# A head's row maxima turned in mid-step, its first product with v in halves, and the maximum of the two halves on GpSimd

## The chip, the core and the metric

The kernel runs on one core of one Trainium2 chip. The core has five engines that run side by side and meet at semaphores: TensorE (PE, with its weight loads shown as PEld), VectorE (DVE), ScalarE (ACT), GpSimd (POOL) and SyncE (SP), which here issues all DMAs. The metric is the device time of one execution in microseconds (us), and lower is better.

## The reference

The layer normalises x (4 sequences of 2048 tokens, 256 wide), and adds to x an attention and a feed-forward branch. The part that matters here is attention with 16 heads of 16 values:

```
qkv = einsum('bld,ed->ble', x, w_qkv);  q, k, v = split(qkv)
q = rope(q);  k = rope(k)
scores = einsum('blhd,bmhd->bhlm', q, k) * scale
attn = softmax(scores, axis=-1)
out = einsum('bhlm,bmhd->blhd', attn, v).reshape(B, L, D)
return einsum('bld,ed->ble', out, w_out)
```

The softmax needs the maximum of each row of scores before its exponentials. There are 4 x 16 = 64 pairs of sequence and head, called heads below, with 2048 x 2048 scores each.

## The kernel before, in words

The first stage (some 540 us) makes normalised x, q, k, v and the feed-forward branch, and stages q and k in HBM as pairs of fp16 numbers. The second stage, attention, is the one that the change touches. It walks 1024 + 32 steps, c = 0, 1, ...; 16 steps (TILES) make a head. Three things run in one step, for three different places in the sequence of tiles:

- The maxima, for tile c. `max_half(c, i, half)` makes 1024 scores of 128 rows in banks 0 and 1 or 2 and 3 of PSUM (two matmuls, L659), and DVE reduces them to one number per row (L1222, `row_max`). PE may write a pair of banks again when DVE has read it (`s1_used`).
- The scores that are turned, for tile c - 19 (FIRST2 = TILES + LAG): four matmuls of 512 columns (L717) with rows added to q, the stabiliser, that subtract the maximum. They go to banks 4, 5, 6 in turn, a ring of three (`take_bank`, `s2_used`), and ACT takes the exponential of each (L828, `probs`).
- The product with v, for tile c - 21: `weigh_v(0)` and `weigh_v(1)`, each 256 columns of four blocks (L699), summed over a head in bank 7.

The order on PE in a step is: max_half 0, scores 0 and 1, weigh_v(0), max_half 1, scores 2 and 3, weigh_v(1). One such half of a step is called a half below. PE works strictly in this order, so an instruction that waits holds all behind it.

Twice per head something else comes in. **Place A** is step c = 16h + 17 (STAB_AT), the second of the next head. DVE has reduced the two halves of `row_max` to `neg_max` (L1212), GpSimd has scaled and split it into three fp16 parts with five small operations (`split_max`, L916 to L927), and PE turns these by a transpose (L678) right behind max_half 0. ACT copies the turned rows to `stabT` (L820), and SP writes them by two DMAs into `q_op` (L438). The scores of step 16h + 19 need them (`stab_loaded`). The transpose counts as two items of the ring of banks (STAB_ITEMS). **Place B** is step 16h + 37 (SAVE_AT): ACT copies the finished sum of head h out of bank 7 (L814, `acc_saved`), before its exponentials of that step. The next head's first product may not write bank 7 before that; in the kernel before it is not cut in two, and stands as one product of 512 columns at the end of the step.

Each engine's part of the program is written out in this order by `step`, without a scheduler.

Of the kernel before, what the change touches and what calls it, by code (L numbers as in the profile page):

```python
# [28 lines left out]
P = 128  # L29
DH = 16  # L30
BANK = 512
# [12 lines left out]
STAB_STEPS = 5  # L44
# [8 lines left out]
UNROLL = SLOTS * TILES  # L53
# [20 lines left out]
def layer_program(nc, x, w_qkv, w_out, w_gate, w_up, w_down, cos_tab, sin_tab, ident_in, out, y_dram, qk_dram, inv_dram):  # L74
# [48 lines left out]
    neg_max = sb(keep, "neg_max", [P, TILES])  # L123
# [3 lines left out]
    unit = sb(keep, "unit", [P, TILES])  # L127
# [149 lines left out]
    max_ready = sem("max_ready")  # L277
# [26 lines left out]

    STAB_ITEMS = 2
    HEAD_ITEMS = 4 * TILES + STAB_ITEMS
    assert HEAD_ITEMS % RING == 0

# [12 lines left out]
    def before(g, at):  # L321

        return min(max((g - at + TILES - 1) // TILES, 0), HEADS)

    def items_before(g):

        return 4 * min(max(g - FIRST2, 0), N1) + STAB_ITEMS * before(g, STAB_AT)

    def extra_items(g):

        return STAB_ITEMS * (head_of(g, STAB_AT) is not None)

    def run_steps(step):

        for c in range(STEPS_B):
            step(c, 0)
# [21 lines left out]
    def _(sp):  # L358
# [71 lines left out]
        def load_stab(hl, i):  # L430
            h = hl + SLOTS * i


            g = TILES * hl + STAB_AT
            sp.wait_ge(s2_used, items_before(g) + STAB_ITEMS + HEAD_ITEMS * SLOTS * i)
            for r in (0, HALF):
                dst = q_op[r + ROWS:r + ROWS + STAB_PARTS, hl % SLOTS, :].rearrange("a (t n) -> a t n", t=TILES)
                sp.dma_start(dst, stabT[:, :]).then_inc(stab_loaded, 16)  # L438
# [31 lines left out]
        for h in range(HEADS):  # L470
            load_stab(h, 0)
# [22 lines left out]
    def _(pe):  # L494
# [131 lines left out]
        pe.wait_ge(b_const, 6)  # L626
# [20 lines left out]
        def max_half(c, i, half):  # L647

            hl, t = divmod(c, TILES)
            if t == 0 and half == 0:  # L650
                pe.wait_ge(qk_loaded[hl % SLOTS], 16 * QK_LOADS * (hl // SLOTS + 1 + i))
            n = 2 * c + half
            if n >= 2:
                pe.wait_ge(s1_used, n - 1 + 2 * UNROLL * i)
# [8 lines left out]
        def step(c, i):  # L663
            item = items_before(c)

            def take_bank(item):

                if item >= RING:
                    pe.wait_ge(s2_used, item - RING + 1 + HEAD_ITEMS * SLOTS * i)
# [12 lines left out]

            def weigh_v(part):

                g3 = g2 - PV_LAG
                if 0 <= g3 < N1:
                    h, t = divmod(g3, TILES)

                    if t == 0 and part == 0:
                        return  # L690
                    if t == 0:
                        pe.wait_ge(v_ready, h + 1 + SLOTS * i)
                        if h >= 1:
                            pe.wait_ge(acc_saved, h + SLOTS * i)
                    if t == 0 or part == 0:
                        pe.wait_ge(s2_used, items_before(c - PV_LAG + 1) + HEAD_ITEMS * SLOTS * i)
                    n0, n1 = (0, BANK) if t == 0 else (part * (BANK // 2), (part + 1) * (BANK // 2))
                    for j in range(4):
                        mm = pe.matmul(bank(7)[32 * j:32 * j + 32, n0:n1], v_op[:, h % 2, t, :],  # L699
                                       probs[:, g3 % PROBS, j * BANK + n0:j * BANK + n1],  # L700
                                       start=(t == 0), stop=(t == TILES - 1 and part == 1), tile_position=(0, 32 * j))
# [3 lines left out]
            for j in range(4):  # L705
                if j == 2:
                    weigh_v(0)
                    if c < N1:
                        max_half(c, i, 1)
                if 0 <= g2 < N1:  # L710
                    h, t = divmod(g2, TILES)
                    if t == 0 and j == 0:
                        pe.wait_ge(stab_loaded, 32 * (h + 1 + SLOTS * i))
# [18 lines left out]
    def _(act):  # L732
# [69 lines left out]
        def step(c, i):  # L802
            item = items_before(c)

            def arrived(item, n=1):
                act.wait_ge(s2_full, item + n + HEAD_ITEMS * SLOTS * i)
# [3 lines left out]
            if h is not None:  # L810
                act.wait_ge(pv_done, TILES * (h + 1 + SLOTS * i))
                if h >= 2:
                    act.wait_ge(o_placed, 64 * (h - 1 + SLOTS * i))
                nc.scalar.activation(acc_sb[:, h % 2, :], bank(7), ACT.Copy).then_inc(acc_saved, 1)  # L814
            h = head_of(c, STAB_AT)
            if h is not None:
                if h >= 1:
                    act.wait_ge(stab_loaded, 32 * (h + SLOTS * i))
                b = arrived(item, STAB_ITEMS)
                nc.scalar.activation(stabT[:, :], bank(b).bitcast(F16)[0:STAB_PARTS * TILES, 0:P], ACT.Copy).then_inc(s2_used, STAB_ITEMS)  # L820
                item += STAB_ITEMS
            g2 = c - FIRST2
            if 0 <= g2 < N1:
                if g2 >= PROBS:
                    act.wait_ge(pv_done, g2 - PROBS + 1 + UNROLL * i)
                for j in range(4):
# [9 lines left out]
    def _(pool):  # L836
# [18 lines left out]
        nc.gpsimd.memset(unit[:, :], 1.0 / STAB_ONE).then_inc(b_const, 1)  # L855
        pool.wait_ge(b_const, 6)
# [55 lines left out]
        def split_max(h, first):  # L912

            n = STAB_STEPS * h
            pool.wait_ge(max_ready, h + 1)
            nc.gpsimd.tensor_tensor(neg_unit[:, :], neg_max[:, :], unit[:, :], ALU.mult).then_inc(stab_step, 1)  # L916
# [3 lines left out]
            pool.wait_ge(stab_step, n + 1)  # L920
            nc.gpsimd.tensor_tensor(stab[:, 0, :], neg_unit[:, :], zero[:, :], ALU.add).then_inc(stab_step, 1)
            pool.wait_ge(stab_step, n + 2)
            nc.gpsimd.tensor_tensor(neg_rem[:, :], neg_unit[:, :], stab[:, 0, :], ALU.subtract).then_inc(stab_step, 1)
            pool.wait_ge(stab_step, n + 3)
# [350 lines left out]
```

## Time and profile before

| what | value |
|---|---|
| median of 3 runs | 3058.35 us (3058.14 to 3059.47) |
| profiled execution | 3054.89 us, span 3053.1 us |
| busy share of the span | PE 95%, DVE 90%, ACT 81%, POOL 14% |
| granted TensorE clock, mean | 0.985 |

Span and busy shares are of the one profiled execution. The records of neighbouring instructions overlap (a reduction has 1.21 us, and the next starts 1.13 us after it), so a busy share near 100% can hide small waits and has to be read beside the starts in the timeline. One head takes about 37.5 us, and almost all of the time from 580 to 2940 us is 63 such periods.

### The profile page before, as it was taken

The page shows a single profiled execution, that of the slowest core. Times are in us where ns is not written, and L with a number is a line of the kernel's source. Part 1 is how long each engine was busy: PE and PEld are TensorE (multiplying, and loading weights), DVE is VectorE, ACT ScalarE, POOL GpSimd, SP SyncE. Part 2 cuts the span into 40 slices and gives each one's busy share as a digit, 9 for nine tenths or more (in the row PEclk, how much of TensorE's full clock was granted, in tenths as well). Part 3 has the DMA queues.
Part 4 walks back from the last instruction along what each step waited for, and adds up shares of the span by engine and source line. Part 5 has one row for each costly group of instructions (what it writes and reads, how often), then busy time and mean ns, then how long its engine had stood idle before and what let it go on. Part 6 is the DMA issues. An engine that isn't in the chain of part 4 may idle for free.

```text
span 3053.1 us, 67192 instructions
## 1 busy us (share of the span) xinstructions
PE 2898.7 (95%) x27416; PEld 1057.6 (35%) x27416; DVE 2743.3 (90%) x3214; ACT 2467.2 (81%) x4609; POOL 429.4 (14%) x672
## 2 busy tenths in 40 slices
PE   4989898799999999999999999999999999999999
PEld 3555555233333333333323333333333333333336
DVE  6767676999999999999999999999999999999952
ACT  4454545399999999999999999999999999999972
POOL 3454545000000000000000000000000000000000
PEclk9999999699999999999999999999999999999999
DMA  2223232011111111111111111111111111111115
GB/s 93 88 77 101 77 109 72 28 28 31 31 31 30 30 30 31 32 32 32 31 31 31 32 31 31 30 30 30 30 30 30 31 30 31 31 30 30 31 61 173
DMA packets 124599, 137.12 MB, mean 45 GB/s; under 512 B 43264, under 2 KB 103296, under 8 KB 124288
## 3 DMA queue, kind: packets, MB, share of 16 engines
q1 hardware_dynamic: 124288, 132.79, 15.4%
q8 instruction: 217, 3.56, 0.5%
q14 instruction: 94, 0.77, 0.1%
HBM read 88.15 MB, written 34.08 MB: 40 GB/s over the span
## 4 chain that ended last, share of the span: by engine, by line
PE 78%; ACT 7%; DVE 6%; POOL 3%; issue 3%; DMA 0%; ACTq 0%; SPq 0%; POOLq 0%; DVEq 0%
PE psum L699 35%; PE psum L659 19%; PE psum L717 16%; ACT probs L828 5%; PE psum L569 3%; PE psum L642 2%; PE psum L592 2%; POOL qk_rot L873 2%; DVE row_max L1222 1%; POOL parts L879 1%; ACT silu L772 1%; DVE y_blk L1143 1%; ACT staged L779 1%; PE psum L584 1%; DVE rot_s L1121 1%
## 5 line engine op out<-in xcount | busy, mean ns | idle before, releaser
L1222 DVE TENSOR_REDUCE row_max<-psum 128x1 f32<-128x1024 f32 x2048 | 2335.8, 1214 | 51.0 <-PE psum L659 51.0
L828 ACT ACTIVATE probs<-psum 128x512 f32<-128x512 f32 x4096 | 2178.3, 597 | 193.6 <-PE psum L717 94.2
L699 PE MATMUL psum<-probs,v_op 128*32 128x256 f32 (+1 forms) x15872 | 1296.4, 398 | 0.0
L717 PE MATMUL psum<-q_op,k_op 51*128 51x512 f16 x4096 | 862.9, 381 | 31.5 <-ACT probs L828 23.3
L659 PE MATMUL psum<-k_op,q_op 48*128 48x512 f16 x4096 | 806.9, 391 | 24.9 <-DVE row_max L1222 20.5
L659 PEld LDWEIGHTS psum<-k_op,q_op 48*128 48x128 f16 x4096 | 196.4, 93 | 895.5 <-issue 526.3
L699 PEld LDWEIGHTS psum<-probs,v_op 128*32 128x32 f32 x15872 | 312.5, 108 | 526.7 <-issue 497.8
L717 PEld LDWEIGHTS psum<-q_op,k_op 51*128 51x128 f16 x4096 | 371.8, 94 | 273.8 <-ACT probs L828 73.6
L941 POOL TENSOR_TENSOR acc_sb<-acc_sb,inv_rows 128x512 f32<-128x512 f32 x64 | 81.6, 1275 | 1914.9 <-DMA inv_rows<-inv_dram 1914.9
L765 ACT ACTIVATE parts<-qk_rot 128x512 f16<-128x512 f32 x64 | 40.3, 630 | 235.7 <-POOL qk_rot L873 235.7
L569 PE MATMUL psum<-xnT,w 128*128 128x512 f16 x768 | 188.2, 393 | 8.3 <-DVE h L1134 8.3
L1134 DVE SCALAR_TENSOR_TENSOR h<-psum,h_fix,silu 128x512 f32<-128x512 f32 x96 | 69.8, 748 | 124.6 <-ACT silu L772 124.5
L561 PE MATMUL psum<-w,xnT 128*128 128x512 f16 (+1 forms) x768 | 129.2, 328 | 6.5 <-POOL lo_max L866 4.1
L569 PEld LDWEIGHTS psum<-xnT,w 128*128 128x128 f16 x768 | 74.8, 101 | 88.2 <-issue 11.4
L873 POOL TENSOR_TENSOR qk_rot<-rot_c,rot_s 128x512 f32<-128x512 f32 x64 | 81.0, 1267 | 170.6 <-DVE rot_s L1121 158.6
L885 POOL TENSOR_TENSOR hT<-h,hT 128x512 f16<-128x512 f32 x80 | 92.6, 1166 | 78.1 <-ACT hT L758 78.1
L1201 DVE TENSOR_TENSOR y_in<-psum,y_in 128x512 f32<-128x512 f32 x32 | 22.1, 692 | 84.7 <-PE psum L642 84.7
L561 PEld LDWEIGHTS psum<-w,xnT 128*128 128x128 f16 x768 | 73.7, 98 | 61.5 <-issue 11.5
L592 PE MATMUL psum<-wdT,hT 128*128 128x256 f16 x768 | 86.7, 273 | 4.8 <-POOL hT L885 4.8
L584 PE MATMUL psum<-identh,parts 128*128 128x128 f16 x512 | 41.7, 228 | 42.7 <-ACT staged L779 42.7
L592 PEld LDWEIGHTS psum<-wdT,hT 128*128 128x128 f16 x768 | 74.3, 98 | 15.8 <-issue 4.9
L772 ACT ACTIVATE silu<-psum,gate_fix 128x512 f32<-128x512 f32 x96 | 64.0, 683 | 13.0 <-PE psum L569 12.1
(102 smaller groups left out, 972.5 us busy)
## 6 DMA issues: line engine op xcount, KB each, us to landing
qk_dram<-staged SPq DMA_DIRECT2D x64, 256.0 KB, 3.1
q_op<-qk_dram SPq DMA_DIRECT2D x128, 128.0 KB
k_op<-qk_dram SPq DMA_DIRECT2D x128, 128.0 KB
x_ln<-in_x SPq DMA_DIRECT2D x16, 512.0 KB, 4.0
x_res<-in_x SPq DMA_DIRECT2D x16, 512.0 KB, 5.0
y_dram<-y_blk SPq DMA_DIRECT2D x16, 512.0 KB, 3.2
k_op<-qk_dram SPq DMA_DIRECT2D x128, 64.0 KB
q_op<-qk_dram SPq DMA_DIRECT2D x128, 64.0 KB
```

What stands on the lines that cost most here:

```text
L561: mm = pe.matmul(dst, xnT[:, xp, c, t * P:(t + 1) * P], wqkvT[:, wp, c, e0:e1], start=(c == 0 and n == 0), stop=(c == KT - 1 and n == 2))
L569: mm = pe.matmul(bank(dst), w[:, wp, c, j * P:(j + 1) * P], xnT[:, xp, c, :], start=(c == 0 and n == 0), stop=(c == KT - 1 and n == len(ff ...
L592: mm = pe.matmul(bank(DOWN_BANK[t], D), hT[:, hp, j, t * P:(t + 1) * P], wdT[:, wp, j, :], start=(j == 0 and n == 0), stop=(j == HT - 1 an ...
L659: mm = pe.matmul(bank(2 * half + j), q_op[r:r + ROWS, s, t * P:(t + 1) * P], k_op[r:r + ROWS, s, cols:cols + BANK], start=True, stop=True)
L699: mm = pe.matmul(bank(7)[32 * j:32 * j + 32, n0:n1], v_op[:, h % 2, t, :], probs[:, g3 % PROBS, j * BANK + n0:j * BANK + n1], start=(t == ...
L717: pe.matmul(bank(b), k_op[r:e, h % SLOTS, t * P:(t + 1) * P], q_op[r:e, h % SLOTS, j * BANK:(j + 1) * BANK], start=True, stop=True).then_i ...
L772: nc.scalar.activation(silu[:, j % 2, :], bank(PAIR_BANK[BLK + j]), ACT.Silu, scale=gate_fix[:, j:j + 1]).then_inc(silu_ready, 1)
L828: nc.scalar.activation(probs[:, g2 % PROBS, j * BANK:(j + 1) * BANK], bank(b), ACT.Exp, scale=to_score).then_inc(s2_used, 1)
L873: nc.gpsimd.tensor_tensor(qk_rot[:, t % 2, :], rot_c[:, t % 2, :], rot_s[:, t % 2, :], ALU.add).then_inc(qk_ready, 1)
L885: nc.gpsimd.tensor_tensor(hT[:, 1, j, :], h32[:, j % H_BUFS, :], hT[:, 0, j, :], ALU.subtract).then_inc(hlo_ready, 1)
L941: nc.gpsimd.tensor_tensor(acc_sb[:, u, :], acc_sb[:, u, :], inv_rows[:, :], ALU.mult).then_inc(o_ready, 1)
L1222: nc.vector.tensor_reduce(row_max[:, hl % 2, t, half:half + 1], psum[:, 2 * half * BANK:(2 * half + 2) * BANK], AX.X, ALU.max).then_inc(s1 ...
```

## The change

At place A the transpose moves from behind max_half 0 to behind max_half 1, that is in front of score 2, and ACT's copy from in front of its first exponential to in front of the third. The transpose is one item of the ring now. At place B the first product with v of a head is in halves like all others, so its first half stands in mid-step, in front of max_half 1, and its waits with it. DVE's `neg_max` is gone: GpSimd makes the maximum of the two halves itself, as first + max(second - first, 0), in four operations where one scaled (`unit`) before, 8 in place of 5 in all. The rest of the diff takes away index terms that are always zero.

```diff
-STAB_STEPS = 5
+STAB_STEPS = 8
...
+    def stab_items(c):
+
+        return 1 if head_of(c, STAB_AT) is not None else 0
+
+    def score_items(c):
+
+        return 4 if 0 <= c - FIRST2 < N1 else 0
...
-            sp.wait_ge(s2_used, items_before(g) + STAB_ITEMS + HEAD_ITEMS * SLOTS * i)
+            sp.wait_ge(s2_used, items_before(g) + score_items(g) // 2 + 1)
...
             if c < N1:
-                max_half(c, i, 0)
-            h = head_of(c, STAB_AT)
-            if h is not None:
-                pe.wait_ge(stab_step, STAB_STEPS * (h + 1 + SLOTS * i))
-                b = take_bank(item)
-                pe.transpose(bank(b).bitcast(F16)[:, 0:P], stab[:, :, :].rearrange("p a t -> p (a t)"),
-                             identh[:, :]).then_inc(s2_full, STAB_ITEMS)
-                item += STAB_ITEMS
+                max_half(c, 0)
...
                     if t == 0 and part == 0:
-                        return
-                    if t == 0:
-                        pe.wait_ge(v_ready, h + 1 + SLOTS * i)
+                        pe.wait_ge(v_ready, h + 1)
                         if h >= 1:
-                            pe.wait_ge(acc_saved, h + SLOTS * i)
-                    if t == 0 or part == 0:
-                        pe.wait_ge(s2_used, items_before(c - PV_LAG + 1) + HEAD_ITEMS * SLOTS * i)
-                    n0, n1 = (0, BANK) if t == 0 else (part * (BANK // 2), (part + 1) * (BANK // 2))
+                            pe.wait_ge(acc_saved, h)
+                    if part == 0:
+                        pe.wait_ge(s2_used, items_before(c - PV_LAG + 1))
+
+                    n0, n1 = part * (BANK // 2), (part + 1) * (BANK // 2)
...
                 if j == 2:
                     weigh_v(0)
                     if c < N1:
-                        max_half(c, i, 1)
+                        max_half(c, 1)
+                    h = head_of(c, STAB_AT)
+                    if h is not None:
+                        pe.wait_ge(stab_step, STAB_STEPS * (h + 1))
+                        b = take_bank(item)
+                        pe.transpose(bank(b).bitcast(F16)[:, 0:P], stab[:, :, :].rearrange("p a t -> p (a t)"),
+                                     identh[:, :]).then_inc(s2_full, 1)
+                        item += 1
...
+            for j in range(4):
+                if j == 2 and stab_items(c):
+                    take_stab(item)
+                    item += 1
...
-            pool.wait_ge(max_ready, h + 1)
-            nc.gpsimd.tensor_tensor(neg_unit[:, :], neg_max[:, :], unit[:, :], ALU.mult).then_inc(stab_step, 1)
+
+            first_half, second_half = row_max[:, h % 2, :, 0], row_max[:, h % 2, :, 1]
+            pool.wait_ge(s1_used, 2 * TILES * (h + 1))
+            nc.gpsimd.tensor_tensor(ahead[:, :], second_half, first_half, ALU.subtract).then_inc(stab_step, 1)
+            nc.gpsimd.tensor_scalar(neg_first[:, :], first_half, -1.0 / STAB_ONE, None, ALU.mult).then_inc(stab_step, 1)
+            pool.wait_ge(stab_step, n + 2)
+            nc.gpsimd.tensor_scalar(neg_more[:, :], ahead[:, :], 0.0, -1.0 / STAB_ONE, ALU.max, ALU.mult).then_inc(stab_step, 1)
+            pool.wait_ge(stab_step, n + 3)
+            nc.gpsimd.tensor_tensor(neg_unit[:, :], neg_first[:, :], neg_more[:, :], ALU.add).then_inc(stab_step, 1)
...
-                dve.wait_ge(s1_used, 2 * TILES * (h + 1 + SLOTS * i))
-                if h >= 1:
-                    dve.wait_ge(stab_step, STAB_STEPS * (h + SLOTS * i))
-                nc.vector.tensor_reduce(neg_max[:, :], row_max[:, h % 2, :, :], AX.X, ALU.max, negate=True).then_inc(max_ready, 1)
+
+            if t == 0 and 2 <= hl < HEADS:
+                dve.wait_ge(stab_step, STAB_STEPS * (hl - 2) + 2)
```

Place A on PE, before (L659 the maxima, L678 the transpose, L717 the scores, L699 the product with v):

```order
L699 MATMUL psum<-probs,v_op 32x256 x4
L659 MATMUL psum<-k_op,q_op 128x512 [waits s1_used]
L659 MATMUL psum<-k_op,q_op 128x512
L678 MATMUL psum<-identh,stab 128x128 [waits s2_used,stab_step]
L717 MATMUL psum<-q_op,k_op 128x512 [waits s2_used] x2
L699 MATMUL psum<-probs,v_op 32x256 [waits s2_used]
L699 MATMUL psum<-probs,v_op 32x256 x3
```

Place A on PE now (L656, L702, L712 and L687 in the same roles):

```order
L656 MATMUL psum<-k_op,q_op 128x512 [waits s1_used]
L656 MATMUL psum<-k_op,q_op 128x512
L712 MATMUL psum<-q_op,k_op 128x512 [waits s2_used] x2
L687 MATMUL psum<-probs,v_op 32x256 [waits s2_used]
L687 MATMUL psum<-probs,v_op 32x256 x3
L656 MATMUL psum<-k_op,q_op 128x512 [waits s1_used]
L656 MATMUL psum<-k_op,q_op 128x512
L702 MATMUL psum<-identh,stab 128x128 [waits s2_used,stab_step]
L712 MATMUL psum<-q_op,k_op 128x512 [waits s2_used] x2
L687 MATMUL psum<-probs,v_op 32x256 x4
```

The transpose has moved one half later, behind the second pair of maxima matmuls.

Place B on PE, before:

```order
L659 MATMUL psum<-k_op,q_op 128x512 [waits s1_used]
L659 MATMUL psum<-k_op,q_op 128x512
L717 MATMUL psum<-q_op,k_op 128x512 [waits s2_used] x2
L659 MATMUL psum<-k_op,q_op 128x512 [waits s1_used]
L659 MATMUL psum<-k_op,q_op 128x512
L717 MATMUL psum<-q_op,k_op 128x512 [waits s2_used] x2
L699 MATMUL psum<-probs,v_op 32x512 [waits s2_used,acc_saved,v_ready]
L699 MATMUL psum<-probs,v_op 32x512 x3
```

Place B on PE now:

```order
L656 MATMUL psum<-k_op,q_op 128x512 [waits s1_used]
L656 MATMUL psum<-k_op,q_op 128x512
L712 MATMUL psum<-q_op,k_op 128x512 [waits s2_used] x2
L687 MATMUL psum<-probs,v_op 32x256 [waits s2_used,acc_saved,v_ready]
L687 MATMUL psum<-probs,v_op 32x256 x3
L656 MATMUL psum<-k_op,q_op 128x512 [waits s1_used]
L656 MATMUL psum<-k_op,q_op 128x512
L712 MATMUL psum<-q_op,k_op 128x512 [waits s2_used] x2
L687 MATMUL psum<-probs,v_op 32x256 x4
```

The wait for `acc_saved` now stands in front of the second pair of maxima matmuls, where before it stood behind them.

## Rows read from the trace of the kernel before

**Rows 1.** Busy time by stretch, in the columns that the first line names.

```profile
core 0: us, PE busy (x) PEld busy (x) DVE busy (x) ACT busy (x) POOL busy (x), PEclk, DMA share, GB/s
1500.00:2000.00 500.00, 493.15 (x5035) 151.70 (x5033) 489.05 (x455) 462.43 (x881) 36.86 (x93) 1.00 0.12 30
```

**Rows 2.** All copies to stabT (L820): duration ns min/median/max, first and last start.

```profile
L820 ACT ACTIVATE stabT<-psum x64: 270/270/271, 580.2 to 2942.4; 48x128 f16<-48x128 f16 x64
```

**Rows 3.** Timeline of DVE: start us, us, engine, line, op, count [idle before].

```profile
1515.11 0.19 DVE L1212 TENSOR_REDUCE neg_max<-row_max 128x16 f32<-128x32 f32 x1
1515.21 3.48 DVE L1222 TENSOR_REDUCE row_max<-psum 128x1 f32<-128x1024 f32 x3
...
1518.93 10.28 DVE L1222 TENSOR_REDUCE row_max<-psum 128x1 f32<-128x1024 f32 x9 [0.25 <-PE psum L659]
...
1529.72 4.62 DVE L1222 TENSOR_REDUCE row_max<-psum 128x1 f32<-128x1024 f32 x4 [0.51 <-PE psum L659]
```

**Rows 4.** Timeline of PE at place A of one head.

```profile
1516.53 0.39 PE L659 MATMUL psum<-k_op,q_op 48*128 48x512 f16 x2
...
1516.95 0.22 PE L678 MATMUL psum<-identh,stab 128*128 128x128 f16 x1
...
1517.61 0.09 PEld L717 LDWEIGHTS psum<-q_op,k_op 51*128 51x128 f16 x1 [0.35 <-ACT stabT L820]
...
1517.93 0.16 PEld L699 LDWEIGHTS psum<-probs,v_op 128*32 128x32 f32 x8 [0.23 <-issue]
...
1518.50 0.10 PEld L659 LDWEIGHTS psum<-k_op,q_op 48*128 48x128 f16 x2 [0.41 <-issue]
...
1518.73 0.38 PE L717 MATMUL psum<-q_op,k_op 51*128 51x512 f16 x2
...
1519.61 0.39 PE L659 MATMUL psum<-k_op,q_op 48*128 48x512 f16 x2
```

**Rows 5.** Timeline of GpSimd and ScalarE at the same place A.

```profile
1508.75 8.38 ACT L828 ACTIVATE probs<-psum 128x512 f32<-128x512 f32 x15
...
1515.37 0.22 POOL L916 TENSOR_TENSOR neg_unit<-neg_max,unit 128x16 f32<-128x16 f32 x1 [4.10 <-DVE neg_max L1212]
...
1515.74 0.22 POOL L921 TENSOR_TENSOR stab<-neg_unit,zero 128x16 f16<-128x16 f32 x1
...
1516.63 0.22 POOL L927 TENSOR_TENSOR stab<-neg_rem,stab 128x16 f16<-128x16 f32 x1
...
1517.29 0.27 ACT L820 ACTIVATE stabT<-psum 48x128 f16<-48x128 f16 x1 [0.17 <-PE psum L678]
...
1517.67 1.08 ACT L828 ACTIVATE probs<-psum 128x512 f32<-128x512 f32 x2
```

**Rows 6.** Timeline at place A of the next head.

```profile
1554.28 0.39 PE L659 MATMUL psum<-k_op,q_op 48*128 48x512 f16 x2
...
1554.61 0.23 PE L678 MATMUL psum<-identh,stab 128*128 128x128 f16 x1
```

**Rows 7.** Timeline of PE and ScalarE at place B.

```profile
1526.35 0.39 PE L659 MATMUL psum<-k_op,q_op 48*128 48x512 f16 x2
...
1526.83 0.60 ACT L814 ACTIVATE acc_sb<-psum 128x512 f32<-128x512 f32 x1
...
1527.30 2.09 ACT L828 ACTIVATE probs<-psum 128x512 f32<-128x512 f32 x4
...
1528.29 0.16 PEld L699 LDWEIGHTS psum<-probs,v_op 128*32 128x32 f32 x8 [0.23 <-issue]
...
1529.29 0.39 PE L659 MATMUL psum<-k_op,q_op 48*128 48x512 f16 x2
```

**Rows 8.** Timeline of SyncE's queue: the two DMAs of stabT at place A.

```profile
1517.59 1.60 SPq L438 DMA_DIRECT2D q_op<-stabT  x2
```

**Rows 9.** Part 6 of the page: DMA issues, KB each, median us from issue to landing.

```profile
sums<-acc_sb SPq DMA_DIRECT2D x256, 2.0 KB, 2.3
```

**Rows 10.** Timeline of the last head's wait for its stabiliser.

```profile
2952.75 0.10 PEld L717 LDWEIGHTS psum<-q_op,k_op 51*128 51x128 f16 x2 [4.42 <-DMA q_op<-stabT]
```

**Rows 11.** Groups of instructions on GpSimd: count, busy us, mean ns, idle before.

```profile
L934 POOL COPY v_op<-v_space 128x256 f32<-128x256 f32 x64 | 25.4, 396 | 0.0
```

More of the change, by code:

```diff
@@ L122, in layer_program @@
     row_max = sb(keep, "row_max", [P, 2, TILES, 2])
-    neg_max = sb(keep, "neg_max", [P, TILES])
+    ahead = sb(keep, "ahead", [P, TILES])
+    neg_first = sb(keep, "neg_first", [P, TILES])
+    neg_more = sb(keep, "neg_more", [P, TILES])
     neg_rem = sb(keep, "neg_rem", [P, TILES])
@@ L319, in sequence_of, with items_before @@
         return n
[L321 to L331, printed above, removed]
+    def stab_items(c):
+        return 1 if head_of(c, STAB_AT) is not None else 0
+    def score_items(c):
+        return 4 if 0 <= c - FIRST2 < N1 else 0
+    ring_items = [0]
+    for c in range(STEPS_B):
+        ring_items.append(ring_items[c] + score_items(c) + stab_items(c))
+    def items_before(c):
+        return ring_items[c]
     def run_steps(step):
         for c in range(STEPS_B):
-            step(c, 0)
+            step(c)
     MAT_MAX_READY, SCALES_READY, DOWN_SPLIT, LO_MAX_READY = 5, 20, 29, 31
@@ L661, in max_half, with step @@
             mm.then_inc(s1_full, 1)
-        def step(c, i):
+        def step(c):
             item = items_before(c)
@@ L700, in weigh_v @@
                                        probs[:, g3 % PROBS, j * BANK + n0:j * BANK + n1],
-                                       start=(t == 0), stop=(t == TILES - 1 and part == 1), tile_position=(0, 32 * j))
+                                       start=(t == 0 and part == 0), stop=(t == TILES - 1 and part == 1), tile_position=(0, 32 * j))
                     if part == 1:
@@ L800, in _, with step, arrived @@
         act.reg_load(to_score, exp_scale[0:1, 1:2].bitcast(I32))
-        def step(c, i):
+        def step(c):
             item = items_before(c)
-            def arrived(item, n=1):
-                act.wait_ge(s2_full, item + n + HEAD_ITEMS * SLOTS * i)
+            def arrived(item):
+                act.wait_ge(s2_full, item + 1)
                 return 4 + item % RING
@@ L810, in step, with take_stab @@
             if h is not None:
-                act.wait_ge(pv_done, TILES * (h + 1 + SLOTS * i))
+                act.wait_ge(pv_done, TILES * (h + 1))
                 if h >= 2:
-                    act.wait_ge(o_placed, 64 * (h - 1 + SLOTS * i))
+                    act.wait_ge(o_placed, 64 * (h - 1))
                 nc.scalar.activation(acc_sb[:, h % 2, :], bank(7), ACT.Copy).then_inc(acc_saved, 1)
-            h = head_of(c, STAB_AT)
-            if h is not None:
+            def take_stab(item):
+                h = head_of(c, STAB_AT)
                 if h >= 1:
[L818 to L821, printed above, removed]
+                    act.wait_ge(stab_loaded, 32 * h)
+                b = arrived(item)
+                nc.scalar.activation(stabT[:, :], bank(b).bitcast(F16)[0:STAB_PARTS * TILES, 0:P], ACT.Copy).then_inc(s2_used, 1)
             g2 = c - FIRST2
[L823 to L826, printed above, removed]
+            if PROBS <= g2 < N1:
+                act.wait_ge(pv_done, g2 - PROBS + 1)
+            for j in range(4):
+                if j == 2 and stab_items(c):
+                    take_stab(item)
+                    item += 1
+                if 0 <= g2 < N1:
                     b = arrived(item)
```

49 lines of the change are left out of this document (19 added, 30 removed).

## The prediction

> **What bounds the kernel now.** I read the busy time by stretch first. In a stretch of 500 us in attention PE is busy for 493, DVE for 489 and ACT for 462 us, at a granted clock of 1.00 [rows 1]. Three engines are nearly full, so no single one can be relieved alone, and a gain can only come from the time in which they wait for each other. Next I took the length of a head from an instruction that occurs once in each: the copies to stabT start from 580.2 to 2942.4 us, 64 of them, so a head takes 2362.2 / 63 = 37.50 us [rows 2].
>
> Then the timeline of PE, to see how much of that is the plain rhythm. From 1519.61 to 1526.35 there are six undisturbed halves, 6.74 us, or 1.123 each [rows 4, 7]. A head has 32, which is 35.94 us, and 1.56 us is left over. It is found at two places. Place A (the turned maxima) goes from 1516.53 to 1519.61, 3.08 us for two halves: 0.83 too long [rows 4]. Place B (the saved sum) goes from 1526.35 to 1529.29, 2.94 us: 0.69 too long [rows 7]. Together 1.52 of the 1.56 us.
>
> DVE tells the same from its side. Its pitch is (10.28 - 1.21) / 8 = 1.134 us, barely above PE's half. From 1515.21 three reductions would reach 1518.61 and the fourth starts at 1518.93, 0.32 late; from 1518.93 nine would reach 1529.14 and the tenth starts at 1529.72, 0.58 late. The neg_max puts another 0.1 to 0.2 us in [rows 3]. So PE and DVE are almost equal, and what is late on PE at A and B arrives on DVE as a wait.
>
> **Place A, before.** PE can't turn the rows until GpSimd has them at 1516.63 + 0.22 = 1516.85; the transpose starts at 1516.95. ACT copies from 1517.29 to 1517.56. Score 1 of that step needs a bank that this copy frees, and its weights load at 1517.61, the product with v at 1517.93, the next maxima at 1518.50 [rows 4, 5].
>
> **Place A, after, in the clock of that head.** Three chains meet, and I lay them side by side.
>
> GpSimd: it starts when the last reduction is through, at 1515.11 at the latest, plus the 0.07 that now lies between the end of neg_max (1515.30) and its start (1515.37): 1515.18. A dependent operation follows the one before after (1516.63 - 1515.74) / 3 = 0.30 us, the one with two waits after 0.37. Eight operations are 6 x 0.30 + 0.37 + 0.22 = 2.39 us: ready at 1517.57 [rows 5]. Two of the eight, tensor_scalar on GpSimd, occur nowhere before. At worst each is as long as the copy of 256 columns, 0.40 in place of 0.22 us, which makes it 1517.93 [rows 11]; at best they save the 0.22 altogether, 1517.13. I take 0.22, the row of the same size.
>
> The Trainium skill, "GPSIMD Engine Reference", section "Engine selection", says that an elementwise maximum belongs on VectorE, since GpSimd is about twice as slow with two inputs. By that rule the move is wrong, and the chain does grow, by three operations. The rows put 0.9 us of it on an engine that is busy for 36.86 of 500 us, and take 0.1 to 0.2 us from one that is busy for 489 [rows 1, 3, 5], so I go by the rows; the rule would matter only if the chain became the last to arrive.
>
> PE: max_half 1 at 1516.53 + 1.12 = 1517.65, the transpose 0.33 us behind it, as where nothing holds it (1554.28 to 1554.61) [rows 6]: 1517.98. GpSimd is there 0.4 us before, or 0.05 in the worst case, so its longer chain is hidden. This is the point of the move: the transpose meets rows that are ready.
>
> ACT: one exponential follows the other after (8.38 - 0.60) / 14 = 0.556 us, and the last of the step before ends at 1517.13. Exponentials 0 and 1 then end at about 1517.75 and 1518.31, and the copy starts at 1517.98 + 0.34 = 1518.32, as the transpose allows [rows 5]. ACT loses no time in waiting for it.
>
> The ring: the transpose takes the place of an item, so score 2 needs exponential 0 and score 3 exponential 1 to be done. Score 3 loads at 1518.31 + 0.05 = 1518.36, the product with v 0.32 later, and the next maxima 0.57 after that: 1519.25, where before it was 1519.61 [rows 4]. Place A gains 0.36 us per head. It isn't free after it: 2.72 - 2.25 = 0.47 us is left, the wait for exponential 1.
>
> **What becomes late.** The copy ends at 1518.59 and not 1517.56, and all after it comes earlier. The DMAs start 0.03 us later, at 1518.62. The second is issued half of 1.60 us behind the first [rows 8], and small DMAs of this queue take 2.3 us to land [rows 9]: 1518.62 + 0.80 + 2.3 = 1521.72. The scores of step 16h + 19 would start at 1519.25 + 2.25 + 0.22 = 1521.72, with weights loaded 0.1 us before, for which the semaphore has to be seen. Before, the landing by the same count was at 1517.59 + 3.1 = 1520.69 and the need at 1519.61 + 2.25 = 1521.86; that slack of 1.2 us shrinks to nothing. I take a stall of 0.12 us, with bounds of 0 and 0.4 (the copy later by most of an exponential).
>
> The Trainium skill, "DMA: Bandwidth & Descriptors", section "Anatomy of one DMA — SWDGE (gpsimd) path", fits about 2.0 us plus bytes / 436e3 for one DMA. By it the 12 KB would land at 1521.45 and PE would not wait, 0.12 us per head or 7 us in all better than my sum; the row of the other small DMA says 2.3, and the trace shows no landing of this one, so I keep the row.
>
> **Place B.** The step now starts at 1519.25 + 0.12 + 6.74 = 1526.11. ACT's copy of bank 7 starts 0.48 us into it and takes 0.60 [rows 7]: 1527.19. The half product waits for that in mid-step, from about 1526.65 to 1527.23, and behind it max_half 1 waits too, which before went ahead. It starts at 1527.23 + 0.57 = 1527.80, and the next step a half later at 1528.92. That is 2.81 us where it was 2.94 [rows 7]: 0.13 gained. The wait for a free score bank (ACT's first exponential only begins at 1527.30 now [rows 7]) has gone, because it lies beneath the wait for the save, but that is as long. DVE gets its data for the held maxima at 1528.23 and would have been free at 1519.68 + 7 x 1.134 = 1527.62: 0.61 us late where it was 0.58 [rows 3]; the following one isn't late any more. So place B is moved about rather than mended.
>
> **The neg_max** is 0.1 to 0.2 us of DVE per head [rows 3]. It is not counted by itself: PE's schedule is the sum, and without that saving DVE would hold it.
>
> **The sum.** 0.36 + 0.13 - 0.12 = 0.37 us per head. Places A and B that are both in the steady stretch: 62. That is 23 us. The last head's stabiliser is waited for 4.42 us anyway, behind other loads [rows 10], so its place A gives nothing. At the first head, where PE runs at half its clock and DVE sets the rhythm, the later copy may cost up to 1 us. I take 22. The profiled execution took 3054.89 us (span 3053.1), so it would come to 3033; the median of the runs shown, 3058.35, is 3.5 above it, and from there I forecast 3036.
>
> **The rivals.**
>
> The landing stays hidden. For it: the 1.2 us of slack before, and a DMA of 12 KB may be as quick as the quickest. Then 0.36 + 0.13 = 0.49 us per head, 30 us: 3028. Less isn't in it, since the wait for exponential 1 and for the save remain.
>
> The gain is eaten by late rows. The stabiliser comes 0.25 to 0.4 us later than I have it (ACT not at once free behind its second exponential, GpSimd's new forms longer), PE waits as much in step 16h + 19, and 0.1 us per head remains: 6 us, 3052. Against it: ACT's copy waited for PE before and not the other way round [rows 5].
>
> It becomes slower. The same wait from a stall of 0.49 us on: that is the point from which the place of the transpose costs more than it gives. At 0.6 us the head is 0.11 longer, 7 us: 3065. It needs the copy to be 0.5 us later than the schedule has it, or landings of 3.6 us, and rows 8 and 9 give 3.1. In that case DVE would also idle three times per head and not twice.
>
> **How the numbers follow.** My forecast has a chance of 0.54 (with its own range from 3029 to 3045, for stalls of 0 to 0.3 us), the hidden landing 0.15, the eaten gain 0.18 and slower 0.13. 0.2%, some 6 us, is what a measurement of this kernel can tell from no change. The first two are faster by more; of the third a good quarter, of the fourth three quarters beyond the bound on the other side. That makes 0.73 faster, 0.17 the same, 0.10 slower. The range runs from 3024, a little under the hidden landing, to 3056, which leaves slower and a part of the eaten gain out.
>
> **What would show it.** The period of the copies to stabT should be 37.1 us. At place A: the transpose starts 0.33 us behind max_half 1 without a wait for GpSimd, the score behind it waits for exponential 1, and the two halves take 2.7 us. The scores of step 16h + 19 show a short wait for the DMA of stabT; none is the first rival, and more than 0.3 us the others. At place B the weights of the product with v wait some 0.6 us for the save, and DVE idles there about as long as before; at A it idles 0.1 us. I am wrong if the transpose waits for GpSimd, if the DMA's wait passes 0.5 us, or if place B is longer than before.

## The result and the profile after

The changed kernel takes 3034.4 us (median of 4 runs, 3032.74 to 3035.68) where the kernel before takes 3058.4; the ratio is 0.9921, with an interval of 0.9903 to 0.9938. Measured again, beside three of the experiments, it was 0.9926 (0.9913 to 0.9940). It is 24 us or 0.8% faster; forecast were 22 us and 3036. One execution of e9_one_item, an experiment below, took 3744.04 us at a granted clock of 0.65 and is left out of its ratio.

The number to compare traces by is the period of a head, since the start of attention alone moves by 2 to 4 us between executions. From 1500 to 2000 us both kernels have a granted clock of 1.00, so the clock doesn't enter into it. The row of all copies to stabT after the change (duration ns min/median/max, first and last start), to hold against [rows 2]:

```profile
L816 ACT ACTIVATE stabT<-psum x64: 270/270/271, 582.6 to 2923.4; 48x128 f16<-48x128 f16 x64
```

(2923.4 - 582.6) / 63 gives 37.16 us with these rounded starts and 37.15 with the unrounded ones, where it was 37.50. The difference, 0.341 us, times 63 makes 21.5 of the 24 us.

Place A in the timeline of PE, GpSimd and ScalarE after the change, to hold against [rows 4, 5]:

```profile
1508.83 0.22 POOL L915 TENSOR_TENSOR ahead<-row_max 128x16 f32<-128x16 f32 x1 [4.90 <-DVE row_max L1222]
1509.02 0.26 POOL L916 TENSOR_SCALAR neg_first<-row_max 128x16 f32<-128x16 f32 x1
...
1509.36 0.28 POOL L918 TENSOR_SCALAR neg_more<-ahead 128x16 f32<-128x16 f32 x1
...
1510.19 0.39 PE L656 MATMUL psum<-k_op,q_op 48*128 48x512 f16 x2
...
1510.98 0.22 POOL L931 TENSOR_TENSOR stab<-neg_rem,stab 128x16 f16<-128x16 f32 x1
...
1511.30 0.39 PE L656 MATMUL psum<-k_op,q_op 48*128 48x512 f16 x2
...
1511.62 0.23 PE L702 MATMUL psum<-identh,stab 128*128 128x128 f16 x1
...
1511.95 0.27 ACT L816 ACTIVATE stabT<-psum 48x128 f16<-48x128 f16 x1
...
1512.03 0.09 PEld L712 LDWEIGHTS psum<-q_op,k_op 51*128 51x128 f16 x1 [0.16 <-ACT probs L827]
...
1512.25 1.60 SPq L435 DMA_DIRECT2D q_op<-stabT  x2
...
1512.92 0.39 PE L656 MATMUL psum<-k_op,q_op 48*128 48x512 f16 x2
...
1515.17 0.39 PE L656 MATMUL psum<-k_op,q_op 48*128 48x512 f16 x2
...
1515.38 0.10 PEld L712 LDWEIGHTS psum<-q_op,k_op 51*128 51x128 f16 x2
```

GpSimd is ready at 1510.98 + 0.22 = 1511.20 and the transpose starts at 1511.62, 0.32 us behind its max_half 1: it waits for nobody. Score 3 waits 0.16 us for an exponential. Place A is 1512.92 - 1510.19 = 2.73 us long. The weights of step 16h + 19 load at 1515.38, 0.21 us behind the maxima and not 0.01 to 0.02 as in other steps: that is when the DMA has landed, 3.13 us after its issue. In this head it costs nothing yet, as the next maxima are not late.

Place B after the change, to hold against [rows 7]:

```profile
1519.66 0.39 PE L656 MATMUL psum<-k_op,q_op 48*128 48x512 f16 x2
...
1519.89 0.38 PE L712 MATMUL psum<-q_op,k_op 51*128 51x512 f16 x2
1520.14 0.60 ACT L809 ACTIVATE acc_sb<-psum 128x512 f32<-128x512 f32 x1
1520.62 1.11 ACT L827 ACTIVATE probs<-psum 128x512 f32<-128x512 f32 x2
...
1520.84 0.64 PE L687 MATMUL psum<-probs,v_op 128*32 128x256 f32 x8 [0.57 <-issue]
1521.41 0.10 PEld L656 LDWEIGHTS psum<-k_op,q_op 48*128 48x128 f16 x2 [0.41 <-DVE row_max L1222]
...
1522.52 0.39 PE L656 MATMUL psum<-k_op,q_op 48*128 48x512 f16 x2
```

The save ends at 1520.74 and the half product starts at 1520.84; PE has stood still for 0.57 us with max_half 1 behind it. The place is 2.86 us long.

DVE in the same stretch, to hold against [rows 3]:

```profile
1497.25 0.24 DVE L1218 RECIPROCAL inv_sum<-sums 128x16 f32<-128x16 f32 x1
1497.41 23.95 DVE L1222 TENSOR_REDUCE row_max<-psum 128x1 f32<-128x1024 f32 x21
1521.85 3.49 DVE L1222 TENSOR_REDUCE row_max<-psum 128x1 f32<-128x1024 f32 x3 [0.48 <-PE psum L656]
```

It runs through place A without a gap, and waits once per head, at place B, for 0.48 us (0.25 + 0.51 before).

Last, five rows of the waits from 1000 to 2500 us after the change (us in total, times, longest):

```profile
PE psum L687 <- issue: 23.4, 41, 0.6
DVE row_max L1222 <- PE psum L656: 22.1, 47, 0.5
PEld psum L702 <- issue: 9.0, 40, 0.2
PEld psum L712 <- ACT probs L827: 8.5, 45, 0.4
PEld psum L712 <- DMA q_op<-stabT: 5.7, 27, 0.5
```

There is no row of the transpose waiting for GpSimd, and one, new, of scores that wait for the DMA of stabT in 27 of 40 heads.

### The profile page after: what moved, and what is told of

It reads as the page before. It is cut to its first block, busy times and chain, and to the rows that moved or that the text cites. A ratio compares the mean times of both kernels' runs of the same rounds, so it can differ in the third digit from the quotient of the medians.

```text
span 3033.6 us, 68340 instructions
## 1 busy us (share of the span) xinstructions
PE 2876.6 (95%) x27928; PEld 1070.3 (35%) x27928; DVE 2733.7 (90%) x3150; ACT 2470.3 (81%) x4609; POOL 475.5 (16%) x863
## 4 chain that ended last, share of the span: by engine, by line
PE 83%; DVE 6%; POOL 3%; issue 2%; ACT 2%; DMA 0%; SPq 0%; POOLq 0%; DVEq 0%; ACTq 0%
PE psum L687 38%; PE psum L656 21%; PE psum L712 17%; PE psum L566 2%; PE psum L639 2%; POOL qk_rot L870 2%; PE psum L589 2%; DVE row_max L1222 2%; POOL parts L876 1%; DVE y_blk L1147 1%; ACT silu L767 1%; ACT staged L774 1%; DVE rot_s L1125 1%; PE psum L581 1%; DVE stats L960 1%
## 5 line engine op out<-in xcount | busy, mean ns | idle before, releaser
L687 PE MATMUL psum<-probs,v_op 128*32 128x256 f32 x16384 | 1310.0, 391 | 35.4 <-issue 35.4
L712 PE MATMUL psum<-q_op,k_op 51*128 51x512 f16 x4096 | 832.6, 381 | 6.1 <-DMA q_op<-stabT 5.6
L656 PE MATMUL psum<-k_op,q_op 48*128 48x512 f16 x4096 | 807.6, 391 | 21.7 <-DVE row_max L1222 20.2
L687 PEld LDWEIGHTS psum<-probs,v_op 128*32 128x32 f32 x16384 | 324.4, 108 | 584.4 <-issue 545.3
L656 PEld LDWEIGHTS psum<-k_op,q_op 48*128 48x128 f16 x4096 | 196.4, 93 | 866.8 <-issue 504.4
L712 PEld LDWEIGHTS psum<-q_op,k_op 51*128 51x128 f16 x4096 | 365.7, 94 | 217.4 <-ACT probs L827 20.6
```

Source lines behind the costliest of these rows:

```text
L656: mm = pe.matmul(bank(2 * half + j), q_op[r:r + ROWS, s, t * P:(t + 1) * P], k_op[r:r + ROWS, s, cols:cols + BANK], start=True, stop=True)
L712: pe.matmul(bank(b), k_op[r:e, h % SLOTS, t * P:(t + 1) * P], q_op[r:e, h % SLOTS, j * BANK:(j + 1) * BANK], start=True, stop=True).then_i ...
```

## The experiments

Each ran five rounds against the kernel before. The lengths of places are medians over heads 1 to 60, taken from the starts of the maxima's matmuls in each trace; at place A 52 to 60 of the 60 heads agree to 0.01 us, so they tell more than the times. "Step 19" is step 16h + 19, undisturbed 2.25 us long.

| run | period, us | place A | step 19, mean | place B | ratio to before (interval) |
|---|---|---|---|---|---|
| before | 37.50 | 3.08 | 2.25 | 2.94 | 1 |
| changed | 37.15 | 2.74 | 2.31 | 2.86 | 0.9921 (0.9903 to 0.9938) |
| e1_whole | 37.26 | 2.74 | 2.32 | 2.94 | 0.9963 (0.9940 to 0.9986) |
| e2_dve_max | 37.14 | 2.73 | 2.30 | 2.86 | 0.9927 (0.9914 to 0.9940) |
| e3_early_turn | 37.56 | 3.21 | 2.25 | 2.86 | 1.0012 (1.0004 to 1.0021) |
| e4_lag4 | 37.09 | 2.74 | 2.26 | | 0.9917 (0.9904 to 0.9930) |
| a2_changed | 37.16 | 2.74 | 2.32 | 2.86 | 0.9926 (0.9913 to 0.9940) |
| e6_score_first | 36.96 | 2.73 | 2.32 | 2.64 | 0.9893 (0.9878 to 0.9908) |
| e7_score_first_lag4 | 36.88 | 2.73 | 2.26 | | 0.9880 (0.9865 to 0.9895) |
| e8_chain_plus3 | 37.68 | 3.00 | 2.57 | 2.86 | 1.0035 (1.0021 to 1.0048) |
| e9_one_item | 37.12 | 2.64 | 2.25 | 2.94 | 0.9904 (0.9889 to 0.9919) |
| e10_one_item_halves | 36.99 | 2.64 | 2.25 | 2.86 | 0.9893 (0.9878 to 0.9908) |
| e11_one_item_score_first | 36.89 | 2.64 | 2.25 | 2.74 | 0.9873 (0.9858 to 0.9888) |
| e5_max_first | 36.96 | 2.73 | 2.32 | 2.64 | 0.9884 (0.9869 to 0.9899) |

With LAG = 4 everything from the scores on lies a step later: place B is step 16h + 38, and its length in the traces is 2.86 us in e4_lag4 and 2.64 in e7_score_first_lag4. The scores that need stabT are then in step 16h + 20, 2.25 us long.

The period runs from the first copy to the last, and so holds the first head too, where single steps of place B and behind it differ by up to 1.7 us between traces: steps 22 and 23 take 3.96 and 3.35 us in e9_one_item, 2.36 and 2.25 in the changed kernel. That puts 0.04 us into the one period and not into the other. Over 60 later heads (steps 48 to 1008) a head takes 37.49 us before, 37.15 in the changed kernel, 37.23 in e1_whole, 37.06 in e9_one_item, 36.98 in e10_one_item_halves and 36.85 in e11_one_item_score_first. These agree with the places.

### The first product whole again

```diff
-                    if t == 0 and part == 0:
-                        pe.wait_ge(v_ready, h + 1)
+                    if t == 0 and part == 0:
+                        return
+                    if t == 0:
+                        pe.wait_ge(v_ready, h + 1)
...
-                    n0, n1 = part * (BANK // 2), (part + 1) * (BANK // 2)
+                    n0, n1 = (0, BANK) if t == 0 else (part * (BANK // 2), (part + 1) * (BANK // 2))
```

> The changed kernel, with the first product of a head with v whole again at the end of its step (one part of the change undone). Theory: place A carries the gain (0.34 us per head) and place B only 0.08 (2.94 us before, 2.86 after), so this loses 62 x 0.08 = 5 us against the changed kernel's 3034.4: 3039. Place B is back at 2.94 us, place A stays at 2.74. Rival: the halves carry as much as the transpose, then half of the 24 us goes: 3046.

3040.94 us, place B back at 2.94 and place A unmoved at 2.74. The period grows by 0.10 us, or 6.5 us in all; over the 60 later heads it is 0.08 us, what place B alone gives. So the halves are worth 5 to 7 us of 24 by the trace, and the theory holds. The times don't settle it alone: the ratio, 0.9963, goes by means, and one execution of 3083.4 us among eleven from 3038 to 3046 makes its interval wide enough for the rival's 3046. By medians this kernel is 7.5 us above e2_dve_max beside it, which is as fast as the changed kernel.

### The maximum of the halves on VectorE again

```diff
-            pool.wait_ge(s1_used, 2 * TILES * (h + 1))
-            nc.gpsimd.tensor_tensor(ahead[:, :], second_half, first_half, ALU.subtract).then_inc(stab_step, 1)
...
+            pool.wait_ge(max_ready, h + 1)
+            nc.gpsimd.tensor_tensor(neg_unit[:, :], neg_max[:, :], unit[:, :], ALU.mult).then_inc(stab_step, 1)
...
+                nc.vector.tensor_reduce(neg_max[:, :], row_max[:, h % 2, :, :], AX.X, ALU.max, negate=True).then_inc(max_ready, 1)
```

> The changed kernel, with the maximum of the two halves on VectorE again (neg_max, five steps on GpSimd in place of eight). Theory: PE's order sets the time and GpSimd's chain is hidden either way, so 3034 to 3038; place A stays at 2.74 us, and DVE idles a little less at place B, since its reduction stands in its way instead. Rival: taking 0.1 to 0.2 us per head from VectorE, whose pitch is the longest, is worth its full price: 62 x 0.15 = 9 us lost, 3044.

3033.41 us with a period of 37.14: no difference. The rival's 3044 lies outside the interval. Freeing the engine with the longest pitch of 0.1 to 0.2 us per head buys nothing: with neg_max back on it, VectorE still idles 0.51 us at place B, where it idles 0.48 us in the changed kernel. That it would idle less, as expected above, is not seen. The third part of the change has no effect in either direction, where it stands with the other two.

### The transpose at its old place, with the long chain

```diff
             if c < N1:
                 max_half(c, 0)
+            h = head_of(c, STAB_AT)
+            if h is not None:
+                pe.wait_ge(stab_step, STAB_STEPS * (h + 1))
...
-                if j == 2 and stab_items(c):
+                if j == 0 and stab_items(c):
```

> The changed kernel, with the transpose and ScalarE's copy back behind max_half 0 and in front of the first exponential; the eight steps on GpSimd, the single ring item and the halved first product stay. Theory: the place is what pays. GpSimd is ready some 1.1 us after the start of that step, the transpose waits for it, and place A becomes about 3.5 to 3.7 us where it is 2.74: 50 to 60 us lost, 3085 to 3095, slower than the kernel before (3058.4). No wait for the DMA of stabT in step 16h + 19. Rival: the ring item that was saved pays and not the place; then 3040 to 3050.

3059.66 us, slower than before by 0.04 to 0.21%. The direction held, the size did not: place A is 3.21 us and not 3.5 to 3.7. The rival's 3040 to 3050 is missed as well. The timeline says why.

```profile
1520.17 0.39 PE L656 MATMUL psum<-k_op,q_op 48*128 48x512 f16 x2
...
1521.22 0.23 PE L675 MATMUL psum<-identh,stab 128*128 128x128 f16 x1 [0.67 <-POOL stab L931]
...
1521.38 0.39 PE L712 MATMUL psum<-q_op,k_op 51*128 51x512 f16 x2
1521.58 0.27 ACT L816 ACTIVATE stabT<-psum 48x128 f16<-48x128 f16 x1 [0.82 <-PE psum L675]
1521.70 0.16 PEld L694 LDWEIGHTS psum<-probs,v_op 128*32 128x32 f32 x8 [0.23 <-issue]
```

The transpose waits for GpSimd until 1.05 us into the step. But then both scores go at once (1521.38, x2) and the product 0.48 us behind the transpose, before the copy to stabT has even ended. In the kernel before, the second score stood until the copy was through (1517.61) and the product came 0.98 us behind the transpose [rows 4]. What had gone was the second item of the ring. I had booked the whole gain of place A to the transpose's new place; this run said that the single item might be the larger part, and e9_one_item puts that to the test.

### One step more between maxima and scores

```diff
-LAG = 3
+LAG = 4
```

> The changed kernel with LAG = 4 in place of 3: the turned scores come one step later after their maxima, so the DMA of stabT has 2.2 us more; one more step at the end of attention. Theory: step 16h + 19 loses 0.07 us on average to that DMA (1 to 2 of them up to 0.4), so 4 us come back and about 2 to 3 us go to the longer end: 3032 to 3034, and no wait of L712 for the DMA. Rival: the wait is covered by VectorE's lag anyway: 3036 to 3037.

3031.91 us with a ratio of 0.9917; steps 19 and 20 of a head, the scores now being in the second of them, are at 2.25 us (2.26 in the mean for step 19), and the period is 0.06 us shorter. The row of scores that wait for the DMA of stabT is gone from the waits of the stretch. The wait was real and cost PE 0.06 us per head, 4 us. The time agrees but doesn't settle it, as the intervals overlap.

### The changed kernel again

> The changed kernel again, on the chip of the next three, to compare them with. Both theories: a ratio of 0.992 to the kernel before, a period of 37.15 us.

3034.3 us, ratio 0.9926, period 37.16.

### Place B: work in front of the wait

```diff
             for j in range(4):
+                if j == 3 and first_v:
+                    weigh_v(0)
                 if j == 2:
-                    weigh_v(0)
+                    if not first_v:
+                        weigh_v(0)
                     if c < N1:
                         max_half(c, 1)
```

> The changed kernel with one difference at place B: the first half of the first product with v, and its wait for the save, stand behind max_half 1 and score 2, not in front of them. Theory: place B is long because PE stands still some 0.6 us behind the save while work that doesn't need bank 7 is queued behind the wait. With it in front, the product still starts at about 1.18 us into the step, but only score 3 and the second half are left after it: 2.56 us in place of 2.86, VectorE gets its maxima in time, 62 x 0.30 = 19 us faster than the changed kernel. Rival: VectorE's pitch is the bound, PE's gain turns into waits for it, and less than a third (6 us) is seen.

3023.9 us, 10 less than the changed kernel beside it, and a period shorter by 0.20 us. Place B is 2.64 us and not 2.56: the timeline of this kernel shows the half product at 1513.83, 1.18 us into the step as expected, but the single score 3 takes 0.32 us until the product behind it (1514.40 to 1514.72), as much as a pair does (0.31 to 0.34).

```profile
1512.65 0.39 PE L656 MATMUL psum<-k_op,q_op 48*128 48x512 f16 x2
...
1513.13 0.60 ACT L813 ACTIVATE acc_sb<-psum 128x512 f32<-128x512 f32 x1
...
1513.83 0.64 PE L687 MATMUL psum<-probs,v_op 128*32 128x256 f32 x8
1514.40 0.09 PEld L716 LDWEIGHTS psum<-q_op,k_op 51*128 51x128 f16 x1 [0.41 <-ACT probs L831]
...
1514.72 0.16 PEld L687 LDWEIGHTS psum<-probs,v_op 128*32 128x32 f32 x8 [0.23 <-issue]
```

DVE's pitch as the bound is ruled out as far as this point.

The same with max_half 1 alone in front of the wait, and score 2 behind it:

```diff
                     if c < N1:
                         max_half(c, 1)
+                    if first_v:
+                        weigh_v(0)
```

> The changed kernel with the first half product behind max_half 1 alone, and score 2 behind it as before: half of the step from the changed kernel to e6_score_first. Theory: VectorE no longer idles at place B, and PE does 0.3 us of work in the wait: 2.64 us or a little more, within 3 us of e6_score_first (3023.9), since score 3 waits for exponential 0 only in neither. Rival: it is score 2 in front of the wait that pays in e6_score_first, and this one stays within 4 us of the changed kernel (3034.3).

3022.76 us, place B 2.64 us, the same as with score 2 moved too. So it is max_half 1 behind the wait that cost the changed kernel 0.22 us of place B per head, and score 2 in front of the wait adds nothing.

### Both together

> The kernel e6_score_first with LAG = 4. Theory: the two add up, 0.06 us per head for the DMA's wait that goes, less 2 to 3 us for the longer end: 1 to 2 us faster than e6_score_first, the fastest of all. Rival: with place B short VectorE binds, and LAG = 4 only adds its longer end: 2 us slower than e6_score_first.

3020.09 us against 3023.9, the period 0.08 us shorter, a little more than the 0.06 of e4_lag4. By the trace it adds up; by the times alone it isn't told apart, as the intervals overlap.

### GpSimd's chain made longer

```diff
+            for extra in range(3):
+                pool.wait_ge(stab_step, n + 4 + extra)
+                nc.gpsimd.tensor_tensor(neg_unit[:, :], neg_first[:, :], neg_more[:, :], ALU.add).then_inc(stab_step, 1)
```

> The changed kernel with neg_unit computed three times more in GpSimd's chain, each waiting for the one before (11 steps in place of 8): 0.89 us longer, with the same result. Theory (the rival of the prediction that ends slower, put to the test): the first 0.35 us are hidden, since GpSimd is ready 0.35 us ahead of the transpose. The other 0.54 delay the transpose; at place A some 0.3 of it are seen (score 3 waits for exponential 1 anyway), and the DMA lands 0.54 later, which adds 0.2 to 0.3 in step 16h + 19. Together 0.5 to 0.6 us per head, 31 to 37 us slower than the changed kernel, slower than the one before. Rival: the chain is hidden throughout, under 5 us.

3067.61 us, 33 more than the changed kernel and slower than the kernel before. Place A grows by 0.26 and step 19 by 0.25 us:

```profile
1523.43 0.22 POOL L934 TENSOR_TENSOR stab<-neg_rem,stab 128x16 f16<-128x16 f32 x1
1523.70 0.10 PEld L702 LDWEIGHTS psum<-identh,stab 128*128 128x128 f16 x1 [0.74 <-POOL stab L934]
...
1527.53 0.10 PEld L712 LDWEIGHTS psum<-q_op,k_op 51*128 51x128 f16 x2 [0.44 <-DMA q_op<-stabT]
```

The rival that ended slower was a sound mechanism: 0.89 us more on an engine busy 10% of the time cost 0.52 us per head (37.68 against 37.16), half at the transpose and half at the DMA that follows it. VectorE waits for the maxima 111 times in 40 heads here, where it waited 47 times in the changed kernel: nearly three times per head, as that rival said.

### One item of the ring, and nothing else of the change

This edit is shown against the kernel before.

```diff
-            sp.wait_ge(s2_used, items_before(g) + STAB_ITEMS + HEAD_ITEMS * SLOTS * i)
+            sp.wait_ge(s2_used, items_before(g) + 1)
...
-                             identh[:, :]).then_inc(s2_full, STAB_ITEMS)
-                item += STAB_ITEMS
+                             identh[:, :]).then_inc(s2_full, 1)
+                item += 1
```

> The kernel before with one thing of the change: the transpose is one item of the ring of score banks and not two. Place, neg_max on VectorE, five steps on GpSimd and the whole first product are as before. Theory now: the run with the early transpose had no wait of a score for ScalarE's copy, so at place A of the kernel before only the wait for GpSimd is due to the place, and the wait of score 1 for the copy is due to the second item. A: transpose at 0.42 us into the step, score 0 0.16 behind it, product 0.32, maxima 0.57, then a half of 1.11: 2.58 us in place of 3.08 (2.74 in the changed kernel). 0.50 us per head, 31 us less than the kernel before: 3027, faster than the changed kernel. Rival: the place is what pays and the second item costs nothing by itself: A stays above 2.9 us, 3050 to 3058.

3030.4 us, ratio 0.9904, period 37.12. Place A is 2.64 us (2.58 expected), shorter than in the changed kernel, and step 19 is undisturbed:

```profile
1508.06 0.39 PE L656 MATMUL psum<-k_op,q_op 48*128 48x512 f16 x2
1508.17 0.22 POOL L929 TENSOR_TENSOR stab<-neg_rem,stab 128x16 f16<-128x16 f32 x1
1508.44 0.10 PEld L675 LDWEIGHTS psum<-identh,stab 128*128 128x128 f16 x1 [0.28 <-POOL stab L929]
...
1508.60 0.49 PE L714 MATMUL psum<-q_op,k_op 51*128 51x512 f16 x2
1508.79 0.27 ACT L818 ACTIVATE stabT<-psum 48x128 f16<-48x128 f16 x1
1509.02 0.16 PEld L696 LDWEIGHTS psum<-probs,v_op 128*32 128x32 f32 x8 [0.23 <-issue]
```

No instruction of PE waits for the copy (1508.79 to 1509.06): the product starts before its end. So the single item alone shortens place A by 0.44 us, more than the 0.34 of the whole change. It is at least as fast as the changed kernel: 0.04 us per head ahead by the period and 0.09 over the 60 later heads, while by the times the intervals overlap.

With the first product in halves as well:

> The kernel e9_one_item with the first product in halves, that is the changed kernel with the transpose at its old place and the short chain on GpSimd. Theory: place B 2.86 in place of 2.94, 5 us less than e9_one_item: 3022, 12 us faster than the changed kernel, and no wait for the DMA of stabT. Rival: VectorE's reductions and neg_max bind by now (32 pitches of 1.13, neg_max, reciprocal: 36.6 us) and PE's gain is not seen: within 3 us of e9_one_item.

3024.9 us, ratio 0.9893, period 36.99, places 2.64 and 2.86: place B gives what it gives in the changed kernel, and VectorE doesn't bind. It is 10 us faster than the changed kernel by the ratios, where 12 were expected, and no score waits for the DMA of stabT.

And with place B as in e6_score_first:

> The kernel e10_one_item_halves with place B as in e6_score_first. Theory: another 0.2 us per head, 12 us: 3010, a period of 36.7 us. Rival: VectorE binds at about 36.8 us per head and half of it is lost: 3016.

3017.76 us, ratio 0.9873 (0.9858 to 0.9888), the fastest median of all (its interval overlaps that of e7_score_first_lag4), and 15 to 16 us less than the changed kernel by the ratios. Place B is 2.74 us here and not 2.64, so about half of the step was lost, as the rival had it. ScalarE runs from place A to the save without a gap, yet the save is not late, 0.47 us into the step. What is late is PE's max_half 1:

```profile
1502.87 0.27 ACT L820 ACTIVATE stabT<-psum 48x128 f16<-48x128 f16 x1
1503.10 9.01 ACT L831 ACTIVATE probs<-psum 128x512 f32<-128x512 f32 x16
1511.99 0.60 ACT L813 ACTIVATE acc_sb<-psum 128x512 f32<-128x512 f32 x1
1512.26 0.10 PEld L656 LDWEIGHTS psum<-k_op,q_op 48*128 48x128 f16 x2 [0.50 <-DVE row_max L1226]
...
1512.80 0.64 PE L694 MATMUL psum<-probs,v_op 128*32 128x256 f32 x8
...
1514.69 2.36 DVE L1226 TENSOR_REDUCE row_max<-psum 128x1 f32<-128x1024 f32 x2 [0.22 <-PE psum L656]
```

PE issues max_half 1 only at 1512.27, behind a wait for DVE, 0.75 us into the step that starts at 1511.52 (0.60 in e6_score_first), and the half product stands 1.28 us into it (1.18 there), 0.21 us behind the end of the save. So it is VectorE that holds PE here, the cause that the rival gave, though it isn't full: it still idles 0.22 us a step later. That its longer backlog comes from neg_max and the shorter place A was not tried by itself.

## Why the prediction was right, and where it wasn't

**Where the time is lost.** PE's rhythm and the two places held: 0.34 + 0.08 - 0.06 us per head, forecast 0.36 + 0.13 - 0.12, account for the measured period within 0.02 us. The nearness of the sum owes something to luck: the stall came out 0.06 us better than forecast and the two places 0.02 and 0.05 us worse, so the errors nearly cancel.

**Place A.** 2.72 us expected, 2.74 measured, with the transpose 0.32 us behind max_half 1 and score 3 held by exponential 1. GpSimd's chain took 1511.20 - 1508.83 = 2.37 us where 2.39 were counted; its tensor_scalar steps, which no row before showed, take 0.26 and 0.28 us. The schedule was right, but the reason given for it was not. "This is the point of the move: the transpose meets rows that are ready" made the place the cause. Six runs of place A part the three edits:

| transpose | items of the ring | GpSimd's chain | place A, us |
|---|---|---|---|
| behind max_half 0 | 2 | 5 steps | 3.08 |
| behind max_half 0 | 1 | 5 steps | 2.64 |
| behind max_half 0 | 1 | 8 steps | 3.21 |
| behind max_half 1 | 1 | 8 steps | 2.74 |
| behind max_half 1 | 1 | 5 steps | 2.73 |
| behind max_half 1 | 1 | 11 steps | 3.00 |

At the old place the single item gains 0.44 us; two items at the new place were not run. The longer chain costs 0.57 at the old place, and the new place hides it for a price of 0.10 there and 0.06 in step 19. The move is needed only because of the work that the same change put on GpSimd, and that work brought nothing (e2_dve_max). I had seen that score 1 waits for the bank that the copy frees, and had STAB_ITEMS in the diff; what I left out was to lay the schedule once with the item alone.

**What becomes late.** The landing was foreseen 3.1 us after the issue; in the head shown it is 3.13, and over 60 heads the weights load 3.10 to 3.39 us after it, 3.19 at the median. So the second DMA is seen some 2.4 us after its own issue, where 2.3 were counted, and the other count of the prediction, 2.03 us and no wait, isn't borne out. The stall was mis-sized all the same, 0.12 us against a mean of 0.06: the sum wants the weights 0.10 us ahead of the matmul, but when they are late the matmul follows them at once (0.004 us), and until 0.2 us behind their usual moment nothing is lost. The longest step 19 is 2.66 us, 0.41 over the undisturbed one and just past the bound of 0.4; PE's weight load stood idle for 0.54 us before it. By the letter that one head in 60 meets the prediction's own sign of being wrong, a wait for the DMA above 0.5 us.

**Place B.** 2.81 expected, 2.86 measured. The term that was off is the release of PE by the save, 0.10 us and not 0.04. "Place B is moved about rather than mended" held: DVE idles 0.48 us there, where it was 0.51. That max_half 1 waits behind the save was seen and priced as harmless; e5_max_first shows that it costs 0.22 us per head.

**The neg_max** counted at nothing was right. DVE's idle time at place A, expected at 0.1 us, is none.

**The rivals.** The wait for the landing is seen in 27 of 40 heads, so it is not hidden; the eaten gain and the slower outcome needed a copy later by 0.25 and 0.5 us, and e8_chain_plus3 shows both what they would have cost and that the changed kernel is some 0.4 us away from the point where the transpose begins to wait.

The 24 us measured are 2.5 more than 63 periods give, and that rest is not explained. The two traces can't place it: the one after the change is shorter by 19.5 us, 21.5 in the periods and 0.5 behind them, less 2.4 in front of the first copy. That start varies by as much anyway (578.7 to 582.6 us in these traces).

## What to carry to other kernels

When one change has several edits at one place, lay the schedule for each alone and not for the sum only: here one edit alone gained at least as much as all three at place A, and a second existed only to hide a third. An item that takes two slots of a ring of buffers makes the next user wait for its consumer; count the slots before moving the instruction. Where an in-order engine must wait, put in front of the wait whatever doesn't need what it waits for, even half a step of it.

## What the runs showed of the hardware

Two things were not expected. Small GpSimd operations of 128x16 elements cost 0.22 us with two tensors and 0.26 to 0.28 us with one tensor and constants, so the form with one input isn't the cheaper one at this size. And on PE a single score matmul of 512 columns took 0.32 us until the product behind it could load, the same as two on separate row groups (0.31 to 0.34), so taking one score of a pair away from behind a wait leaves the time of the pair there: e6_score_first and e5_max_first both have 2.64 us at place B.
